# Padding between the weight sub-tiles, and feed-forward matmuls that read their tokens backwards

## The chip, the cores and the metric

One core of a Trainium2 chip runs the whole program. The metric is the device time of one execution in microseconds (us). TensorE is written PE in the views of the profile, its weight loads PEld; VectorE is DVE, ScalarE is ACT, GpSimd is POOL and SyncE is SP.

## The reference

Input `x` has 8 sequences of 512 tokens with 256 features. Two residual blocks follow each other. The first is a recurrent block (projections, 8 exponential moving averages along the tokens, gates, a layer norm). The second is a mixture of feed-forward networks (FFNs), in which nearly all of the arithmetic lies:

```python
def _dense(x, wi, wo):
    return jax.nn.relu(x @ wi) @ wo          # 256 -> 1024 -> 256
s0 = _dense(hidden_states, share_wi[0], share_wo[0])
s1 = _dense(hidden_states, share_wi[1], share_wo[1])
s2 = _dense(hidden_states, share_wi[2], share_wo[2])
...
expert_out = out_a * wa + out_b * wb         # two of four experts, picked for each sequence
g = jax.nn.softmax(jax.nn.relu(gi @ gate_w1) @ gate_w2, axis=-1)
out = expert_out * g[:, 0, None, None] + s0 * g[:, 1, None, None] + s1 * g[:, 2, None, None] + s2 * g[:, 3, None, None]
```

Each sequence thus passes five FFNs: three shared ones and two experts. Everything is float32.

## The kernel before

The work goes sequence by sequence. Features lie on the 128 partitions (256 features are `CT` = 2 tiles), tokens along the free dimension. Each float32 operand is split into a high and a low part of type float32r, and a product is three matmuls: high by high, low weights by high data, high weights by low data.

An FFN of one sequence has 8 slots (`TPF`), one for each 128 of the 1024 hidden features; five FFNs make 40 slots (`SLOTS`). A slot has an `up` and a `down`, and `mixture` of the TensorE program (line 744) runs `up` two slots (`LAG`) ahead of `down`.

- `up` (line 668) makes one bank of `ps_up` with six matmuls. For each of two feature tiles, line 695 multiplies the high weights and line 696 the low weights with `x2_hi`; `up_rest` (line 665) multiplies the high weights with `x2_lo`, twice. All 512 tokens are the moving operand.
- ScalarE applies relu and writes `hid_hi` (line 1065, function `relu`), VectorE writes the rest `hid_lo` (line 1306).
- `down` (line 705) makes both banks of `ps_down` with six matmuls: lines 737 and 738 with `hid_hi` for each of two output tiles, then line 741 twice with `hid_lo`. Again the tokens are the moving operand. (Line 730 does one of these in the last slot.)

The last sequence runs two of the FFNs in halves of 256 tokens (`LAST_PASSES`); there the weights of the last slots lie in `xg_hi_all`, `xg_lo_all`, `ct_hi`, `ct_lo`, `wc_hi`, `wc_lo` and `x2_*_all` (`again_wi`, `again_wo`), and one pass writes to `ps_aux`.

Before each matmul TensorE loads 128x128 weights, beside the matmul before it. The weights of half an FFN are a unit: `wi` and `wo` have two buffers of [high part, low part] each, and a part has `CT * UF` = 1024 or `UT * E` = 1024 elements in a partition (4096 bytes). SyncE's queue brings them from a scratch in DRAM that holds the split weights: `load_wi` (line 532) and `load_wo` (line 539), one transfer of 8192 bytes in a partition each. During the first sequence the weights are split on the chip and stored there by `keep_wi` (line 505) and `keep_wo` (line 511).

The recurrent block of the next sequence is woven between the slots by plans (`PLAN_TENSOR` and its like, lines 50 to 120), through `ps_aux` and with weights in `wc_hi` and `wc_lo`. Its moving operands `xg_hi` and `xg_lo` start after a margin of `EDGE` = 128 zero elements in each feature tile; one element of the margin is read (`gate_product`, line 770). For the second sequence the same product reads `x1_hi` and `x1_lo` from the tail of `x2_hi_all` and `x2_lo_all`, with a margin `EDGE1` = 16.

The tensors lie in a partition one after the other in the order of lines 193 to 250. From their sizes: the first is at byte 1152, `wi` at 17536, `wo` at 33920, `hid_hi` at 66688, `wc_hi` at 83072, `x2_hi_all` at 151680, `x2_lo_all` at 160384, `xg_hi_all` at 177280, and the last ends at 228996 (a partition has 229376 bytes). Every start named here leaves 128 when it is divided by 512, and so does each tile of 128 weights and each row of 512 tokens in `wi`, `wo`, `hid_hi`, `hid_lo`, `x2_hi`, `x2_lo`, `xg_hi` and `xg_lo`. The exceptions are `x1_hi` and `x1_lo`: their two feature tiles start at remainders 192 and 256.

Of the kernel before, what the change touches and what calls it, by code (L numbers as in the profile page):

```python
# [10 lines left out]
F32R = mybir.dt.float32r  # L11
# [3 lines left out]
P = 128  # L15
B, T, E = 8, 512, 256
CT = E // P
# [9 lines left out]
UF = F // 2  # L27
UT = UF // P
# [4 lines left out]
NU = 4  # L33
# [66 lines left out]
for _d in range(D):  # L100
# [25 lines left out]
               (4, slice(HALF, T)), (3, slice(HALF, T)))  # L126
LAST_SLOTS = len(LAST_PASSES) * TPF
AGAIN = LAST_SLOTS - TPF
EDGE = 128
EDGE1 = 16  # L130

AUX_BANKS = {"mod_hidden": (0,), "mod": (1,), "gate_hidden": (0,)}
GATING = {"gate_hidden", "gate_part_hi", "gate_part_lo", "gate_logits", "gate_exp", "gate_part", "gate_soft",
          "mix0", "mix1", "mix2", "mix3", "store", "store0", "store1", "final_scale", "final_expert_a", "final_expert_b",
          *(f"final_early{i}" for i in range(NS + 1)), *(f"final_late{i}" for i in range(NS))}


def later(count):
# [32 lines left out]
def build(nc, x, w_ctx, params, types_row, types_all, shared_wi, shared_wo, expert_wi, expert_wo,  # L171
# [3 lines left out]
    split_wi = nc.dram_tensor("split_wi", [KEPT, 2, P, 2 * CT * UF], F32, kind="Internal").ap()  # L175
    split_wo = nc.dram_tensor("split_wo", [KEPT, 2, P, 2 * UT * E], F32, kind="Internal").ap()

    with ExitStack() as ctx:
        def sb(name, shape, dt=F32):
            return ctx.enter_context(nc.sbuf_tensor(name, shape, dt))  # L180
# [7 lines left out]

        raw_wi = sb("raw_wi", [P, 2, CT * UF])
        raw_wo = sb("raw_wo", [P, 2, UT * E])  # L190
        wi = sb("wi", [P, 2, 2, CT * UF], F32R)
        wo = sb("wo", [P, 2, 2, UT * E], F32R)
        ex = sb("ex", [P, 2, 2, CT * UF])
        hid_hi = sb("hid_hi", [P, NU, T], F32R)
        hid_lo = sb("hid_lo", [P, NU, T], F32R)
# [55 lines left out]
        ps_up = [ctx.enter_context(nc.psum_tensor(f"ps_up{i}", [P, T], F32)) for i in range(NU)]  # L251
# [130 lines left out]
        def f32(ap):  # L382
            return ap.bitcast(F32)
# [34 lines left out]
        def half(h):  # L418
            return slice(h * HALF, (h + 1) * HALF)

        def col(c, i=0):
            return par[:, c + i:c + i + 1]

# [48 lines left out]
        def _(sp):  # L472
# [26 lines left out]
            def kept_place(split, u):  # L499
                ffn, half = u // 2, u % 2  # L500
                if ffn < NS:
                    return split[ffn, half]
                return split[bass.ds(expert["now"] + ffn, 1), half].rearrange("o p f -> (o p) f")

            def keep_wi(u):

                sp.wait_ge(wi_ready, u + 1)
                sp.dma_start(kept_place(split_wi, u), f32(wi[:, u % 2, :, :]).rearrange("p s f -> p (s f)"))\
                    .then_inc(wi_kept[u % 2], 16)

            def keep_wo(u):

                sp.wait_ge(wo_ready, u + 1)
                sp.dma_start(kept_place(split_wo, u), f32(wo[:, u % 2, :, :]).rearrange("p s f -> p (s f)"))\
                    .then_inc(wo_kept[u % 2], 16)

            def split_source(kept, of, b, u):
# [14 lines left out]
            def load_wi(b, u):  # L532
                b, u, count, buf = unit_of(b, u)
                source = split_source(wi_kept, split_wi, b, u)

                sp.wait_ge(up_done, (count - 1) * UT)
                sp.dma_start(f32(wi[:, buf, :, :]).rearrange("p s f -> p (s f)"), source).then_inc(wi_landed[buf], 16)

            def load_wo(b, u):
                b, u, count, buf = unit_of(b, u)  # L540
                source = split_source(wo_kept, split_wo, b, u)

                sp.wait_ge(down_done, (count - 1) * UT)
                sp.dma_start(f32(wo[:, buf, :, :]).rearrange("p s f -> p (s f)"), source).then_inc(wo_landed[buf], 16)

            def load_again_wi(half):

# [107 lines left out]
        def _(pe):  # L655
# [6 lines left out]
            def up_rest(ps, w_hi, parity, tokens):  # L662

                for c in range(CT):
                    mm = pe.matmul(ps, w_hi[c], x2_lo[:, parity, c, tokens], start=False, stop=c == CT - 1)  # L665
                return mm

            def up(b, at, parity, tokens=None, done=True, last=False):

                k, part = slot_of(at, last)  # L670
                opens = tokens is not None
                tokens = tokens or part
                u, j = k // UT, k % UT
                if k == 0 and tokens.stop == T and not opens:
                    pe.wait_ge(x2_hi_ready, b)
                if j == 0 and b == 0:
                    pe.wait_ge(wi_ready, u + 1)
                if j == 0 and b > 0 and at < SLOTS:
                    pe.wait_ge(wi_landed[u % 2], 16 * ((b - 1) * (UNITS // 2) + u // 2 + 1))
                if j == 0 and at >= AGAIN:  # L680
                    pe.wait_ge(again_loaded[u % 2], 64)

                ps = ps_up[at % NU][:, tokens]

                def weights(c):
                    if at >= AGAIN:
                        return [w[:, c, j * P:(j + 1) * P] for w in again_wi[u % 2]]
                    cols = slice(c * UF + j * P, c * UF + (j + 1) * P)
                    return wi_hi[:, u % 2, cols], wi_lo[:, u % 2, cols]

                for c in range(CT):
                    w_hi, w_lo = weights(c)
                    if opens and k == 0:
                        pe.wait_ge(open_x2_hi, tokens.start // HALF * CT + c + 1)
                    pe.matmul(ps, w_hi, x2_hi[:, parity, c, tokens], start=c == 0, stop=False)  # L695
                    pe.matmul(ps, w_lo, x2_hi[:, parity, c, tokens], start=False, stop=False)  # L696
                if opens and tokens.start == 0:
                    return
                elif k == 0 and tokens.stop == T:
                    pe.wait_ge(x2_split, b + 1)  # L700
                mm = up_rest(ps, [weights(c)[0] for c in range(CT)], parity, tokens)
                if done:
                    mm.then_inc(up_done, 1)

            def down(b, at, last=False):

                k, tokens = slot_of(at, last)
                u, j = k // UT, k % UT
                ffn = k // TPF
                if j == 0 and b == 0:  # L710
                    pe.wait_ge(wo_ready, u + 1)
                if j == 0 and b > 0 and at < SLOTS:
                    pe.wait_ge(wo_landed[u % 2], 16 * ((b - 1) * (UNITS // 2) + u // 2 + 1))
                w_hi, w_lo = again_wo[u % 2] if at >= AGAIN else (wo_hi[:, u % 2, :], wo_lo[:, u % 2, :])
                pe.wait_ge(hid_hi_ready, b * SLOTS + (at + 1))
                banks = []
                for c in range(CT):
                    cols = slice(j * E + c * P, j * E + (c + 1) * P)

                    if k % TPF == 0 and ffn == 0 and later(b * 2):  # L720
                        pe.wait_ge(experts_ready, b * 2 - (1 - c))
                    if k % TPF == 0 and ffn > 0 and at < SLOTS:
                        pe.wait_ge(y_ready, b * 8 + (2 * ffn - 1 + c))
                    if at == AGAIN:
                        pe.wait_ge(experts_ready, b * 2 + 1 + c)
                    start, stop = k % TPF == 0, k % TPF == TPF - 1
                    bank = ps_down[c][:, tokens]
                    if at == LAST_SLOTS - 1 and c == 1:
                        pe.wait_ge(hid_ready, b * SLOTS + (at + 1))
                        pe.matmul(banks[0][0], banks[0][1], hid_lo[:, at % NU, tokens], start=False, stop=True)\  # L730
                            .then_inc(last_down, 1)
                        banks = []
                    if SLOTS <= at < AGAIN:
                        bank = ps_aux[1][:, c * HALF:(c + 1) * HALF]
                        start, stop = start and c == 0, stop and c == CT - 1
                    banks.append((bank, w_hi[:, cols], stop))
                    pe.matmul(bank, w_hi[:, cols], hid_hi[:, at % NU, tokens], start=start, stop=False)  # L737
                    pe.matmul(bank, w_lo[:, cols], hid_hi[:, at % NU, tokens], start=False, stop=False)  # L738
                pe.wait_ge(hid_ready, b * SLOTS + (at + 1))
                for bank, w, stop in banks:  # L740
                    mm = pe.matmul(bank, w, hid_lo[:, at % NU, tokens], start=False, stop=stop)  # L741
                mm.then_inc(down_done, 1)

            def mixture(b, k, parity, last):
# [212 lines left out]
            def opening():  # L957
# [53 lines left out]
                    up(0, k, 0, half(0), done=False)  # L1011
                pe.wait_ge(open_x2_split, 1)
                for k in range(LAG):
                    up_rest(ps_up[k][:, half(0)], [wi_hi[:, 0, c * UF + k * P:c * UF + (k + 1) * P] for c in range(CT)], 0, half(0))
                open_turn_back(1)
                next_x_terms(ps_aux[1], W_SOMA, 1).then_inc(open_x1_done, 1)
                for k in range(LAG):
# [847 lines left out]
```

## Time and profile before

| | |
|---|---|
| time, median of 2 runs | 1045.24 us (1045.14 and 1045.34) |
| span of the profiled execution, first to last instruction | 1044.1 us |
| its mean granted TensorE clock | 0.999 of full |
| TensorE matmul busy | 1036.7 us, 99% |
| TensorE weight loads busy | 861.1 us, 82% |
| VectorE, ScalarE, GpSimd busy | 756.8, 405.0, 16.3 us |
| moved by DMA | 223.02 MB, mean 214 GB/s |

The profiled execution has its span in the page; its own time outside the profiler is not listed, and the two times shown stand 1.0 and 1.2 us above the span. A matmul's recorded duration holds the time in which its results drain, so matmuls overlap in the records and the distance from one start to the next is what counts. Where the timeline merges two or more matmuls (x2), the second starts inside the row.

### The profile page before, as it was taken

The page shows a single profiled execution, that of the slowest core. Times are in us where ns is not written, and L with a number is a line of the kernel's source. Part 1 is how long each engine was busy: PE and PEld are TensorE (multiplying, and loading weights), DVE is VectorE, ACT ScalarE, POOL GpSimd, SP SyncE. Part 2 cuts the span into 40 slices and gives each one's busy share as a digit, 9 for nine tenths or more (in the row PEclk, how much of TensorE's full clock was granted, in tenths as well). Part 3 has the DMA queues.
Part 4 walks back from the last instruction along what each step waited for, and adds up shares of the span by engine and source line. Part 5 has one row for each costly group of instructions (what it writes and reads, how often), then busy time and mean ns, then how long its engine had stood idle before and what let it go on. Part 6 is the DMA issues. An engine that isn't in the chain of part 4 may idle for free.

```text
span 1044.1 us, 12751 instructions
## 1 busy us (share of the span) xinstructions
PE 1036.7 (99%) x4850; PEld 861.1 (82%) x4850; DVE 756.8 (72%) x1260; ACT 405.0 (39%) x663; POOL 16.3 (2%) x26
## 2 busy tenths in 40 slices
PE   8999999999999999999999999999999999999998
PEld 5688888888888888888888888888888888888898
DVE  6989977799547986389764996559955599545236
ACT  8654555423443234422344223433334432423232
POOL 1200000000000000000000000000000000000000
PEclk9999999999999999999999999999999999999999
DMA  5388999786354754466544664546645465355582
GB/s 213 121 313 275 312 356 356 282 324 240 131 192 167 257 181 162 162 238 210 197 164 163 231 235 152 185 162 242 208 154 201 163 235 204 146 201 191 203 323 90
DMA packets 38302, 223.02 MB, mean 214 GB/s; under 512 B 4514, under 2 KB 5282, under 8 KB 16610
## 3 DMA queue, kind: packets, MB, share of 16 engines
q1 hardware_dynamic: 35938, 209.63, 56.1%
q0 software_dynamic: 2304, 12.58, 3.2%
q8 instruction: 38, 0.62, 0.2%
q14 instruction: 22, 0.18, 0.0%
HBM read 188.51 MB, written 33.69 MB: 213 GB/s over the span
## 4 chain that ended last, share of the span: by engine, by line
PE 96%; DMA 2%; DVE 2%; issue 0%; SPq 0%; ACT 0%; DVEq 0%
PE ps_up L665 14%; PE ps_up L695 14%; PE ps_up L696 14%; PE ps_down L737 14%; PE ps_down L741 14%; PE ps_down L738 14%; PE ps_aux L658 2%; PE ps_aux L659 2%; PE ps_aux L660 2%; DMA wi<-split_wi 1%; DVE y L1633 1%; PE ps_aux L837 1%; PE ps_aux L834 1%; PE ps_aux L833 1%; PE ps_aux L822 1%; PE ps_aux L818 1%
## 5 line engine op out<-in xcount | busy, mean ns | idle before, releaser
L1065 ACT ACTIVATE hid_hi<-ps_up 128x512 fp32r<-128x512 f32 (+1 forms) x336 | 193.5, 576 | 507.8 <-PE ps_up L665 507.6
L1306 DVE SCALAR_TENSOR_TENSOR hid_lo<-ps_up,hid_hi 128x512 fp32r<-128x512 f32 (+1 forms) x336 | 220.1, 658 | 228.9 <-ACT hid_hi L1065 227.5
L695 PE MATMUL ps_up<-x_hi_all,wi 128*128 128x512 f32 (+1 forms) x660 | 250.8, 382 | 0.4 <-DMA wi<-split_wi 0.4
L696 PE MATMUL ps_up<-x_hi_all,wi 128*128 128x512 f32 (+1 forms) x660 | 249.9, 380 | 0.0
L737 PE MATMUL ps_down<-hid_hi,wo 128*128 128x512 f32 (+1 forms) x640 | 245.3, 384 | 0.1
L738 PE MATMUL ps_down<-hid_hi,wo 128*128 128x512 f32 (+1 forms) x640 | 245.1, 384 | 0.0
L665 PE MATMUL ps_up<-x_lo_all,wi 128*128 128x512 f32 (+1 forms) x660 | 197.4, 380 | 0.2 <-DVE x_lo_all L1297 0.2
L741 PE MATMUL ps_down<-hid_lo,wo 128*128 128x512 f32 (+1 forms) x640 | 193.9, 384 | 0.0
L695 PEld LDWEIGHTS ps_up<-x_hi_all,wi 128*128 128x128 f32 x660 | 124.1, 188 | 24.1 <-DMA wi<-split_wi 0.8
L696 PEld LDWEIGHTS ps_up<-x_hi_all,wi 128*128 128x128 f32 x660 | 124.1, 188 | 23.0
L665 PEld LDWEIGHTS ps_up<-x_lo_all,wi 128*128 128x128 f32 x660 | 122.0, 188 | 24.3 <-DVE x_lo_all L1297 0.4
L737 PEld LDWEIGHTS ps_down<-hid_hi,wo 128*128 128x128 f32 x640 | 120.2, 188 | 24.7 <-issue 0.2
L738 PEld LDWEIGHTS ps_down<-hid_hi,wo 128*128 128x128 f32 x640 | 120.2, 188 | 23.5
L741 PEld LDWEIGHTS ps_down<-hid_lo,wo 128*128 128x128 f32 x640 | 119.0, 188 | 24.0 <-DVE hid_lo L1306 0.3
L1416 DVE TENSOR_TENSOR_SCAN trace<-alpha,trace 128x512 f32<-128x512 f32 x98 | 119.1, 1216 | 0.0
L1450 DVE SCALAR_TENSOR_TENSOR trace<-modb,blend_w,gates 128x512 f32<-128x512 f32 x98 | 68.9, 744 | 0.0
L1459 DVE TENSOR_TENSOR temporal<-trace,temporal 128x512 f32<-128x512 f32 x98 | 62.1, 676 | 0.0
L1373 DVE SCALAR_TENSOR_TENSOR x<-y,g,x 128x512 f32<-128x512 f32 x56 | 38.9, 746 | 0.2
L658 PE MATMUL ps_aux<-xg_hi_all,wc_hi 128*128 128x512 f32 x88 | 34.5, 392 | 0.0
L659 PE MATMUL ps_aux<-xg_lo_all,wc_hi 128*128 128x512 f32 x88 | 34.3, 389 | 0.0
L660 PE MATMUL ps_aux<-xg_hi_all,wc_lo 128*128 128x512 f32 x88 | 34.2, 389 | 0.0
L1078 ACT ACTIVATE y<-ps_down 128x512 f32<-128x512 f32 x48 | 26.1, 596 | 18.5 <-PE ps_down L741 18.5
(248 smaller groups left out, 855.1 us busy)
## 6 DMA issues: line engine op xcount, KB each, us to landing
wi<-split_wi SPq DMA_DIRECT2D x70, 1024.0 KB, 4.8
wo<-split_wo SPq DMA_DIRECT2D x70, 1024.0 KB, 4.9
modb<-mod_scratch SPq DMA_DIRECT2D x28, 512.0 KB, 4.6
split_wi<-wi SPq DMA_DIRECT2D x10, 1024.0 KB, 7.3
split_wo<-wo SPq DMA_DIRECT2D x10, 1024.0 KB, 7.6
xt<-in_x SPq DMA_DIRECT2D x8, 512.0 KB, 5.8
split_wi<-ex POOLq DMA_DIRECT2D x4, 1024.0 KB, 8.6
split_wo<-ex POOLq DMA_DIRECT2D x4, 1024.0 KB, 6.0
```

The costliest lines, as they stand in the source:

```text
L658: pe.matmul(ps, w_hi, x_hi, start=start, stop=False)
L665: mm = pe.matmul(ps, w_hi[c], x2_lo[:, parity, c, tokens], start=False, stop=c == CT - 1)
L695: pe.matmul(ps, w_hi, x2_hi[:, parity, c, tokens], start=c == 0, stop=False)
L696: pe.matmul(ps, w_lo, x2_hi[:, parity, c, tokens], start=False, stop=False)
L737: pe.matmul(bank, w_hi[:, cols], hid_hi[:, at % NU, tokens], start=start, stop=False)
L738: pe.matmul(bank, w_lo[:, cols], hid_hi[:, at % NU, tokens], start=False, stop=False)
L741: mm = pe.matmul(bank, w, hid_lo[:, at % NU, tokens], start=False, stop=stop)
L1065: act.activation(hid_hi[:, k % NU, tokens], ps_up[k % NU][:, tokens], ACT.Relu).then_inc(hid_hi_ready, 1)
L1306: dve.scalar_tensor_tensor(hid_lo[:, k % NU, tokens], ps_up[k % NU][:, tokens], 0.0, f32(hid_hi[:, k % NU, tokens]), ALU.max, ALU.subtract ...
L1416: scan = dve.tensor_tensor_scan(trace_of(d)[:, c, :], alpha[:, d:d + 1].broadcast_to([P, T]), trace_of(d)[:, c, :], 0.0, ALU.mult, ALU.add)
L1450: dve.scalar_tensor_tensor(trace_of(d)[:, c, :], modb[:, d // 2 % 2, d % 2, :], blend_w[:, c, d:d + 1], gates[:, c, :], ALU.mult, ALU.mult ...
L1459: dve.tensor_tensor(temporal[:, c, :], trace[:, c, :], temporal[:, c, :], ALU.add).then_inc(ema_sum, 1)
```

## The change

`wi` gets 32 unused elements (128 bytes) after each part, `wo` 16 (64 bytes). The margin `EDGE` shrinks from 128 to 96. The transfers that fill or store `wi` and `wo` move two pieces of 4096 bytes in a partition in place of one of 8192. All FFN matmuls take the token slice with step -1 from the last to the first: `up` so leaves `ps_up` in reversed order, relu and its rest keep that order, and `down` reverses it again. Where the first sequence's opening does halves of the tokens, `up` writes to the mirrored half of the bank.

```diff
-EDGE = 128
+EDGE = 96
+WI_PAD = 32
+WO_PAD = 16
...
+def back(tokens):
+
+    return slice(tokens.stop - 1, tokens.start - 1 if tokens.start else None, -1)
...
-        wi = sb("wi", [P, 2, 2, CT * UF], F32R)
-        wo = sb("wo", [P, 2, 2, UT * E], F32R)
+        wi = sb("wi", [P, 2, 2, CT * UF + WI_PAD], F32R)[:, :, :, 0:CT * UF]
+        wo = sb("wo", [P, 2, 2, UT * E + WO_PAD], F32R)[:, :, :, 0:UT * E]
...
+        def mirrored(tokens):
+            return slice(T - tokens.stop, T - tokens.start)
...
-                sp.dma_start(f32(wi[:, buf, :, :]).rearrange("p s f -> p (s f)"), source).then_inc(wi_landed[buf], 16)
+                sp.dma_start(f32(wi[:, buf, :, :]), source.rearrange("p (s f) -> p s f", s=2)).then_inc(wi_landed[buf], 16)
...
-                    mm = pe.matmul(ps, w_hi[c], x2_lo[:, parity, c, tokens], start=False, stop=c == CT - 1)
+                    mm = pe.matmul(ps, w_hi[c], x2_lo[:, parity, c, back(tokens)], start=False, stop=c == CT - 1)
...
-                ps = ps_up[at % NU][:, tokens]
+                ps = ps_up[at % NU][:, mirrored(tokens) if opens else tokens]
...
-                    pe.matmul(ps, w_hi, x2_hi[:, parity, c, tokens], start=c == 0, stop=False)
-                    pe.matmul(ps, w_lo, x2_hi[:, parity, c, tokens], start=False, stop=False)
+                    pe.matmul(ps, w_hi, x2_hi[:, parity, c, back(tokens)], start=c == 0, stop=False)
+                    pe.matmul(ps, w_lo, x2_hi[:, parity, c, back(tokens)], start=False, stop=False)
...
-                    pe.matmul(bank, w_hi[:, cols], hid_hi[:, at % NU, tokens], start=start, stop=False)
-                    pe.matmul(bank, w_lo[:, cols], hid_hi[:, at % NU, tokens], start=False, stop=False)
+                    pe.matmul(bank, w_hi[:, cols], hid_hi[:, at % NU, back(tokens)], start=start, stop=False)
+                    pe.matmul(bank, w_lo[:, cols], hid_hi[:, at % NU, back(tokens)], start=False, stop=False)
...
-                    mm = pe.matmul(bank, w, hid_lo[:, at % NU, tokens], start=False, stop=stop)
+                    mm = pe.matmul(bank, w, hid_lo[:, at % NU, back(tokens)], start=False, stop=stop)
```

`keep_wi`, `keep_wo` and `load_wo` change as `load_wi` does, and line 730 as the last line shown.

## Rows read from the trace of the kernel before

**Rows 1.** The page: busy time of each engine, the 40 slices, the clock
```profile
PE 1036.7 (99%) x4850; PEld 861.1 (82%) x4850; DVE 756.8 (72%) x1260; ACT 405.0 (39%) x663; POOL 16.3 (2%) x26
...
PE   8999999999999999999999999999999999999998
...
PEclk9999999999999999999999999999999999999999
```

**Rows 2.** The page: the chain that ended last, its shares by engine
```profile
PE 96%; DMA 2%; DVE 2%; issue 0%; SPq 0%; ACT 0%; DVEq 0%
```

**Rows 3.** Groups by line, TensorE: count, busy us, mean ns, idle before
```profile
L695 PE MATMUL ps_up<-x_hi_all,wi 128*128 128x512 f32 (+1 forms) x660 | 250.8, 382 | 0.4 <-DMA wi<-split_wi 0.4
L696 PE MATMUL ps_up<-x_hi_all,wi 128*128 128x512 f32 (+1 forms) x660 | 249.9, 380 | 0.0
L737 PE MATMUL ps_down<-hid_hi,wo 128*128 128x512 f32 (+1 forms) x640 | 245.3, 384 | 0.1
...
L658 PE MATMUL ps_aux<-xg_hi_all,wc_hi 128*128 128x512 f32 x88 | 34.5, 392 | 0.0
...
L738 PE MATMUL ps_aux<-hid_hi,wo 128*128 128x256 f32 x16 | 4.2, 284 | 0.0
...
L922 PE MATMUL ps_up<-ident,modb 128*128 128x128 f32 x32 | 4.0, 273 | 0.0
...
L696 PE MATMUL ps_up<-x_hi_all,ct_lo 128*128 128x256 f32 x8 | 2.1, 283 | 0.0
```

**Rows 4.** Timeline of TensorE, 498.5 to 501.8 us: start, duration
```profile
498.32 0.39 PE L696 MATMUL ps_up<-x_hi_all,wi 128*128 128x512 f32 x1
498.55 0.39 PE L695 MATMUL ps_up<-x_hi_all,wi 128*128 128x512 f32 x1
...
501.49 0.39 PE L696 MATMUL ps_up<-x_hi_all,wi 128*128 128x512 f32 x1
```

**Rows 5.** Timeline of TensorE in the opening: float32 matmuls, not float32r
```profile
22.23 1.91 PE L922 MATMUL ps_up<-ident,modb 128*128 128x128 f32 x16
...
31.04 7.03 PE L893 MATMUL ps_down<-y,gw 128*128 128x512 f32 x16
...
37.48 0.59 PE L893 MATMUL ps_down<-y,gw 128*128 128x512 f32 x1
```

**Rows 6.** Timeline of TensorE around the product with `x1` (margin 16)
```profile
60.40 0.40 PE L658 MATMUL ps_aux<-x_hi_all,wc_hi 128*128 128x512 f32 x1
60.63 0.40 PE L659 MATMUL ps_aux<-x_lo_all,wc_hi 128*128 128x512 f32 x1
60.87 0.39 PE L660 MATMUL ps_aux<-x_hi_all,wc_lo 128*128 128x512 f32 x1
...
65.94 0.39 PE L695 MATMUL ps_up<-x_hi_all,wi 128*128 128x512 f32 x1
```

**Rows 7.** DMA issues by destination: count, KB each, median us to landing
```profile
wi<-split_wi SPq DMA_DIRECT2D x70, 1024.0 KB, 4.8
wo<-split_wo SPq DMA_DIRECT2D x70, 1024.0 KB, 4.9
modb<-mod_scratch SPq DMA_DIRECT2D x28, 512.0 KB, 4.6
```

**Rows 8.** The chain that ended last, 205 to 230 us: the one late load
```profile
211.87 0.47 PE ps_up L665 x2
212.34 0.02 issue
212.35 12.53 DMA wi<-split_wi
```

**Rows 9.** Waits: ScalarE for TensorE, VectorE for ScalarE: us, times, longest
```profile
ACT hid_hi L1065 <- PE ps_up L665: 507.6, 297, 6.7
DVE hid_lo L1306 <- ACT hid_hi L1065: 227.5, 152, 4.5
```

More of the change, by code:

```diff
@@ L507, in keep_wi @@
                 sp.wait_ge(wi_ready, u + 1)
-                sp.dma_start(kept_place(split_wi, u), f32(wi[:, u % 2, :, :]).rearrange("p s f -> p (s f)"))\
+                sp.dma_start(kept_place(split_wi, u).rearrange("p (s f) -> p s f", s=2), f32(wi[:, u % 2, :, :]))\
                     .then_inc(wi_kept[u % 2], 16)
@@ L513, in keep_wo @@
                 sp.wait_ge(wo_ready, u + 1)
-                sp.dma_start(kept_place(split_wo, u), f32(wo[:, u % 2, :, :]).rearrange("p s f -> p (s f)"))\
+                sp.dma_start(kept_place(split_wo, u).rearrange("p (s f) -> p s f", s=2), f32(wo[:, u % 2, :, :]))\
                     .then_inc(wo_kept[u % 2], 16)
@@ L543, in load_wo @@
                 sp.wait_ge(down_done, (count - 1) * UT)
-                sp.dma_start(f32(wo[:, buf, :, :]).rearrange("p s f -> p (s f)"), source).then_inc(wo_landed[buf], 16)
+                sp.dma_start(f32(wo[:, buf, :, :]), source.rearrange("p (s f) -> p s f", s=2)).then_inc(wo_landed[buf], 16)
             def load_again_wi(half):
@@ L729, in down @@
                         pe.wait_ge(hid_ready, b * SLOTS + (at + 1))
-                        pe.matmul(banks[0][0], banks[0][1], hid_lo[:, at % NU, tokens], start=False, stop=True)\
+                        pe.matmul(banks[0][0], banks[0][1], hid_lo[:, at % NU, back(tokens)], start=False, stop=True)\
                             .then_inc(last_down, 1)
@@ L1013, in opening @@
                 for k in range(LAG):
-                    up_rest(ps_up[k][:, half(0)], [wi_hi[:, 0, c * UF + k * P:c * UF + (k + 1) * P] for c in range(CT)], 0, half(0))
+                    up_rest(ps_up[k][:, half(1)], [wi_hi[:, 0, c * UF + k * P:c * UF + (k + 1) * P] for c in range(CT)], 0, half(0))
                 open_turn_back(1)
```

## The prediction

> **What bounds the kernel now.** I read the page first: TensorE is busy for 1036.7 of 1044.1 us, in every slice from the second to the last but one at nine tenths or more, at full clock (2.4 GHz) [rows 1]. The chain that ended last is TensorE for 96% [rows 2]. ScalarE waits for TensorE's `up` 297 times and 507.6 us in all, and VectorE in turn for ScalarE [rows 9]: they are ahead and wait. So the time is the number of matmuls times their distance, and I asked the timeline for that distance. From 498.32 to 501.49 us there are 14 steps, 226.4 ns each [rows 4] (with the rounding of the starts, 226 to 227; I use 226.7). 512 columns at 2.4 GHz are 213.3 ns. So each float32r matmul costs some 13.4 ns more than its columns. Float32 matmuls cost less on top: each of their passes runs at half the column rate, and 15 steps from 31.04 to 37.48 us are 429.3 ns each, where 512 columns at 1.2 GHz are 426.7; the 128-column ones have 15 steps in 1.91 - 0.27 us (one takes 273 ns), 109 ns each, against 106.7 [rows 3, 5]. They have the same weight loads, and only some 2.5 ns on top. So about 10.9 ns of a float32r matmul seem to come from two streams that both read the same memory, the tokens at double rate and the next weights beside them. This surplus is what the change can move, in either sense.
>
> A third row says that the surplus depends on where the operands lie. The product with `x1` has 24 matmuls of 512 columns between 60.40 and 65.94 us [rows 6]. That is 230.8 ns each, 4.1 more than in rows 4. They differ in one thing that I can see: their tokens start 64 or 128 bytes (one element less in half of them) off the remainder (mod 512) that all weights share.
>
> **How many matmuls it touches.** Lines 695, 696 and 665 have 660 each, lines 737, 738 and 741 640 each: 3900; the smaller groups of these lines, with other weights or banks, are three of 16 and twelve of 8, of which one each is shown, 144 together [rows 3]. That is 4044 of 4850 records, 2028 of `up` and 2016 of `down`, most with 512 columns.
>
> **The change part by part.**
>
> Padding. I worked out the new places from the sizes. `wi` still starts at remainder 128 (mod 512); its four parts now start at 128, 256, 384 and 0. `wo` starts at 128 too (`wi` grew by 512), its parts are at 128, 192, 256 and 320. `wo` grew by 256, so all behind it, `hid_hi`, `hid_lo`, `x2_hi`, `x2_lo`, `wc_hi` and `wc_lo`, moves to 384. If only the remainder mod 256 matters, a token row (128) agrees with high `wi` in both buffers and high `wo` in the first. High weights are 4 of 6 loads. Then a third of `up` (676) and two thirds of `down` (1344) are off, 2020 matmuls, at 4.1 ns [rows 6]: +8.3 us. If it is mod 512, only high `wi` of the second buffer agrees: two thirds of `up` and all of `down`, 3368, +13.8 us. I take 8.3, because the rows show a cost for shifts of 64 and 128 bytes and none for 256. From below: nothing excludes that a distance that no row has costs less than the present one; the nearest row is the float32 surplus of 2.5 ns [rows 5], 10.9 ns less on 4044: -44 us. From above, 230.8 need not be the worst.
>
> Margin. `xg_hi` and `xg_lo` have three lines with 88 matmuls, 264 [rows 3]. Their rows now start at 256 and 128 (high) and at 0 and 384 (low), against weights at 384: half of them off mod 256, 132 at 4.1 ns, +0.5 us. The shrink is what lets the padding fit: 768 bytes more would end the last tensor at 229764, past 229376; with 512 fewer it ends at 229252.
>
> Backwards tokens. No row has a moving operand with step -1. What it adds in instructions is nothing. Its price has bounds far apart. Below: it could turn a crossing of the two streams into a parallel run and save the 10.9 ns, the same -44 us as above (not twice). Above: the row at half column rate [rows 5], 429 instead of 227 ns, +202 ns on 4044 (less on the few with 256 columns), about +800 us. I take zero, the row nearest to it being the same matmul read forwards [rows 4]: four consecutive elements are the same bytes in either order, and the bank that is written and relu see no change of order in their own addresses.
>
> As to that, the Trainium skill ("SBUF — State Buffer", Specifications) says that SBUF works in 16-byte cachelines and an access stream keeps its rate with two hits in each. A reversed float32 row has four, so by that rule the reversal is free; no row of this trace shows a reversed stream.
>
> Transfers. The count of DMAs and their place on SP's queue stay. Each `wi` or `wo` load has twice the pieces at half the size. Loads of 1024 KB in 8192-byte pieces land in 4.8 us; `modb` moves 512 KB in pieces of 2048 bytes in 4.6 [rows 7]. If 4096-byte pieces moved at that lower rate, a load would take at most 9.2 us. A buffer is refilled while the four slots of the other one run, 12 matmuls each at 0.227 us: 10.9 us. So it stays hidden at either end in the steady part. It isn't hidden where the queue is full: at 212 us a load took 12.53 us and TensorE idled 0.4 us [rows 3, 8]. A few per cent more there costs another 0.3 us; the bound, if the early loads all slow down, is some 4 us. I take 0.3. If the surplus falls instead, a slot shrinks by 0.13 us of 2.72 and the same covers hold.
>
> Sum: 1044.1 + 8.3 + 0.5 + 0.3 = 1053.2 us of span. The median of the runs stands 1.1 us above the span of the profiled execution; with that, 1054.3 us.
>
> **The rivals.**
>
> *The surplus goes.* The weights and the tokens now run so that they seldom want the same bytes of a line. For it: the surplus exists, it belongs to the double-rate stream, and it moves with the operands' places [rows 4 to 6]. Against it: the places now differ from part to part, so no single good distance is chosen, and the only other distances that the trace has cost more. Price: between all of it, 4044 x 10.9 = 44 us (1001 us), and half of it (1023 us); 1012 us in the middle.
>
> *Nothing moves.* The surplus is a fixed price of a float32r weight swap, and the 4.1 ns of rows 6 have another cause in that busy stretch. Price: the 0.3 us of transfers, 1045.5 us. In the Trainium skill ("TensorE: Matmul & The Clock Gate", Part 2) the engine has one read port for the moving operand and an independent one for the weights, so that a load takes no bandwidth from the running matmul; by that rule the places and the direction are nothing and the time stays. Its 2.5 ns on top of N/2.4 would also be the whole surplus: float32 passes agree with it (429 ns), float32r ones, at 226.7, don't.
>
> *The streams run together (slower).* If the weights are read from the last column to the first, the reversed tokens now move in the same direction at twice the pace, catch up with them, and queue behind them instead of crossing. Where: in the first half of every FFN matmul. Price: a load of 128 columns reads for some 107 ns [rows 5]; tokens held to half rate for all of it lose 53 ns in each matmul, +216 us; held for a quarter of it, 13.3 ns, +54 us, 1099 us. It decides from 5.2 ns in each matmul on (21 us). For it: the surplus behaves like a conflict. Against it: no row tells in which order weights are read.
>
> *Backward reads at half rate (slower).* The double rate may need two neighbours in rising order. Then 512 columns take 429 ns as in rows 5, and the time is some 1045 + 800 = 1845 us. This is the case in which the change doesn't do what it says. For it: only that no row shows the opposite.
>
> **How the numbers follow.** Misplaced parts at the old surplus, my forecast: 0.32, of which 0.30 ends below 1066 us. Surplus goes: 0.30, of which 0.28 is over 2% (below 1024.3 us). Nothing moves: 0.11. Streams together: 0.20. Half rate: 0.07. Over 2% is about what a measurement of this kernel can tell from no change. Faster: 0.28. Slower: 0.02 + 0.20 + 0.07 = 0.29. Within 2%: 0.30 + 0.02 + 0.11 = 0.43. The forecast's own range is 1047 to 1066 us. The range for 8 in 10 leaves out the half rate, the upper half of the streams together and the very end of the surplus: 1003 to 1110 us.
>
> **What would show it.** In the changed profile the distance of FFN matmuls in the timeline is the whole answer. Right: 226.7 ns where a matmul's tokens and the next weights agree mod 256, and some 231 elsewhere, different from part to part. Wrong: one distance near 216 to 221 everywhere (surplus gone), 227 everywhere (nothing moves), 240 or more (together), 429 (half rate). For the smaller terms: PE idle before line 695 from `wi` loads above 1 us would show the transfers mis-sized, and a landing time of `wi` far from 5 us too.

## The result and the profile after

The changed kernel takes 1069.9 us (median of 2 runs, 1069.4 and 1070.4) against 1045.24 before: ratio 1.0238, with its 95% interval 1.0208 to 1.0267. It is slower by over 2%. I had forecast 1054.3 us and "within 2%" as the likeliest outcome; the time lies in the stated range of 1003 to 1110 us. It is just above the part of it that I had for my forecast (1047 to 1066 us), and where I had put "the streams run together" (21 us and more above the old time), but the mechanism is neither's, as the experiments show.

The page of the kernel after answers to [rows 1, 2]:

```profile
PE 1060.5 (99%) x4850; PEld 861.8 (81%) x4850; DVE 758.0 (71%) x1260; ACT 404.6 (38%) x663; POOL 16.3 (2%) x26
...
PE   8999999999999999999999999999999999999998
...
PEclk9999999999999999999999999999999999999999
...
PE 97%; DVE 2%; DMA 1%; issue 0%; SPq 0%; ACT 0%; DVEq 0%
```

TensorE is what bounds it, now too, at the same clock, with the same 4850 matmuls. Its busy time grew by 23.8 us (1060.5 - 1036.7), the span by 23.6 (1067.7 - 1044.1). So the waits didn't grow in sum: the matmuls themselves stand further apart. Nor is it the loads' own length: PEld is 861.8 us against 861.1.

The timeline of TensorE after, in the same stretch as [rows 4] (line 705 is line 695 of before; all lines behind the diff's first part are shifted by 10):

```profile
505.72 0.40 PE L705 MATMUL ps_up<-x_hi_all,wi 128*128 128x512 f32 x1
...
508.52 0.40 PE L705 MATMUL ps_up<-x_hi_all,wi 128*128 128x512 f32 x1
...
514.12 0.40 PE L705 MATMUL ps_up<-x_hi_all,wi 128*128 128x512 f32 x1
```

From one slot's first matmul to the next one's are 12 steps: 2.80 us, 233.3 ns each, and 8.40 us for 36. Inside the slots it is the same, whichever part of `wi` or `wo` is loaded. I had asked the timeline to choose between 226.7 ns mixed with 231 by part, one value of 216 to 221, 227 everywhere, and 240 or more. It shows one value everywhere in this stretch, but 233, which is none of the four.

The view of stretches says the same for the middle of the run. Columns: stretch, its length, then busy us and number of instructions of PE, PEld, DVE, ACT, POOL, the clock, the DMA share and GB/s. First before, then after:

```profile
400.00:1000.00 600.00, 599.93 (x2739) 499.53 (x2738) 407.11 (x673) 208.96 (x333) 0.00 (x0) 1.00 0.54 193
```

```profile
400.00:1000.00 600.00, 600.00 (x2661) 487.33 (x2660) 406.01 (x675) 204.90 (x323) 0.00 (x0) 1.00 0.53 187
```

2739 matmuls in 600 us became 2661, 219.1 ns each became 225.5 (all kinds and sizes together).

Where the whole difference lies can be added up. With the shapes kept apart, the groups of the six FFN lines hold 3 x 604 and 3 x 608 = 3636 matmuls of 512 columns, in both kernels. Over the pairs of these that follow each other directly in the records with less than 250 ns between their starts (3575 before, 3577 after) the mean distance from start to start is 226.93 ns before and 233.46 after. The difference times 3636 is 23.7 us, as much as the whole loss. The FFN passes with 256 columns didn't grow (119.8 ns before, 119.0 after). I use this mean, "the mean distance", for every kernel below; it moves by 0.1 to 0.2 ns with the limit at which a step counts as a wait, so hundredths mean nothing in it. What is left nearly cancels: the other products with 512 columns, untouched by the reversal, take 1 us more, and the steps above 250 ns, which hold the waits, change by less than that in sum.

The smaller terms, in the groups by line and in the DMA issues (columns: count, KB each, median us to landing) of the kernel after:

```profile
L705 PE MATMUL ps_up<-x_hi_all,wi 128*128 128x512 f32 (+1 forms) x660 | 255.8, 390 | 0.4 <-DMA wi<-split_wi 0.4
```

```profile
wi<-split_wi SPq DMA_DIRECT2D x70, 1024.0 KB, 5.2
wo<-split_wo SPq DMA_DIRECT2D x70, 1024.0 KB, 5.2
```

The smaller pieces cost a load 0.3 to 0.4 us [rows 7]. TensorE idles 0.4 us for `wi`, the same sum as before [rows 3], but for another load. The late one of before, at 212 us [rows 8], no longer delays it. The chain that ended last has a new one, in the last sequence, where the FFNs run in halves:

```profile
1021.18 6.55 DMA wi<-split_wi
1027.73 0.04 issue
1027.77 0.39 PE ps_up L705
```

Four slots of 12 matmuls with 256 columns last 5.7 us there (119.0 ns each), and this load took 6.55. pad_only, below, waits at the same place (0.3 us for `wi`, behind a load of 6.52 us); back_only, whose loads move in pieces of 8192 bytes, has no wait for `wi` at all. So the smaller pieces aren't quite hidden.

ScalarE and VectorE still wait for TensorE (536.9 us in 303 waits, against 507.6 in 297 [rows 9]). The product with `x1` is unmoved, 24 steps in 5.54 us, 230.8 ns, as in [rows 6]:

```profile
60.16 0.40 PE L668 MATMUL ps_aux<-x_hi_all,wc_hi 128*128 128x512 f32 x1
...
65.70 0.40 PE L705 MATMUL ps_up<-x_hi_all,wi 128*128 128x512 f32 x1
```

### The profile page after: what moved, and what is told of

Its sections match the earlier page's. It is cut to its first block, busy times and chain, and to the rows that moved or that the text cites. A ratio compares the mean times of both kernels' runs of the same rounds, so it can differ in the third digit from the quotient of the medians.

```text
span 1067.7 us, 12751 instructions
## 1 busy us (share of the span) xinstructions
PE 1060.5 (99%) x4850; PEld 861.8 (81%) x4850; DVE 758.0 (71%) x1260; ACT 404.6 (38%) x663; POOL 16.3 (2%) x26
## 4 chain that ended last, share of the span: by engine, by line
PE 97%; DVE 2%; DMA 1%; issue 0%; SPq 0%; ACT 0%; DVEq 0%
PE ps_up L705 14%; PE ps_up L675 14%; PE ps_up L706 14%; PE ps_down L747 14%; PE ps_down L748 14%; PE ps_down L751 14%; PE ps_aux L668 2%; PE ps_aux L670 2%; PE ps_aux L669 2%; DVE y L1643 1%; PE ps_aux L843 1%; PE ps_aux L847 1%; PE ps_aux L844 1%; DMA wi<-split_wi 1%; PE ps_aux L827 1%; PE ps_aux L828 1%
## 5 line engine op out<-in xcount | busy, mean ns | idle before, releaser
L1075 ACT ACTIVATE hid_hi<-ps_up 128x512 fp32r<-128x512 f32 (+1 forms) x336 | 193.5, 576 | 537.3 <-PE ps_up L675 536.9
L705 PE MATMUL ps_up<-x_hi_all,wi 128*128 128x512 f32 (+1 forms) x660 | 255.8, 390 | 0.4 <-DMA wi<-split_wi 0.4
L706 PE MATMUL ps_up<-x_hi_all,wi 128*128 128x512 f32 (+1 forms) x660 | 254.8, 388 | 0.0
L747 PE MATMUL ps_down<-hid_hi,wo 128*128 128x512 f32 (+1 forms) x640 | 250.3, 392 | 0.1
L748 PE MATMUL ps_down<-hid_hi,wo 128*128 128x512 f32 (+1 forms) x640 | 250.0, 392 | 0.0
L675 PE MATMUL ps_up<-x_lo_all,wi 128*128 128x512 f32 (+1 forms) x660 | 201.7, 388 | 0.2 <-DVE x_lo_all L1307 0.2
L751 PE MATMUL ps_down<-hid_lo,wo 128*128 128x512 f32 (+1 forms) x640 | 198.2, 392 | 0.0
```

The source lines that it names most:

```text
L675: mm = pe.matmul(ps, w_hi[c], x2_lo[:, parity, c, back(tokens)], start=False, stop=c == CT - 1)
L705: pe.matmul(ps, w_hi, x2_hi[:, parity, c, back(tokens)], start=c == 0, stop=False)
L706: pe.matmul(ps, w_lo, x2_hi[:, parity, c, back(tokens)], start=False, stop=False)
L747: pe.matmul(bank, w_hi[:, cols], hid_hi[:, at % NU, back(tokens)], start=start, stop=False)
L748: pe.matmul(bank, w_lo[:, cols], hid_hi[:, at % NU, back(tokens)], start=False, stop=False)
L751: mm = pe.matmul(bank, w, hid_lo[:, at % NU, back(tokens)], start=False, stop=stop)
```

## The experiments

My theory after the result: reading the tokens from the last to the first has a price of its own, 6.6 ns in each 512-column matmul, and the padding adds little to it. The rivals: the padding costs it and the order of the tokens is free (my forecast, with more parts misplaced than I counted); or the reversed tokens run in the same direction as the weight reads and so get in their way ("the streams run together").

### First: the two halves of the change

**pad_only** takes the reversal out of the changed kernel:

```diff
-    return slice(tokens.stop - 1, tokens.start - 1 if tokens.start else None, -1)
+    return tokens
...
-            return slice(T - tokens.stop, T - tokens.start)
+            return tokens
```

> The changed kernel with its padding and margin, but tokens read forwards. Theory P (the places cost, the direction nothing): 230 to 233.3 ns from one FFN matmul to the next, and 1060 to 1070 us. Theory D (the direction costs, the places nothing): 226.7 ns and 1045 to 1047 us. My forecast's own step (226.7 ns where tokens and weights agree mod 256, 230.8 elsewhere): two distances, and 1054 us.

**back_only** takes the padding out:

```diff
-EDGE = 96
-WI_PAD = 32
-WO_PAD = 16
+EDGE = 128
+WI_PAD = 0
+WO_PAD = 0
```

> The changed kernel with no padding and the margin of 128, tokens read backwards. Theory P: 226.7 ns and 1045 us. Theory D: 233.3 ns and 1069 to 1070 us. If the padding was meant to soften what the direction costs: more than 233.3 ns, over 1070 us.

Measured: pad_only 1060.7 us, ratio 1.0143 [1.0126, 1.0159]; back_only 1067.9 us, ratio 1.0214 [1.0197, 1.0231]; before, on the same chip, 1045.6. The timelines of pad_only and, under it, back_only:

```profile
504.96 0.39 PE L705 MATMUL ps_up<-x_hi_all,wi 128*128 128x512 f32 x1
...
506.35 0.39 PE L747 MATMUL ps_down<-hid_hi,wo 128*128 128x512 f32 x1
...
507.75 0.39 PE L705 MATMUL ps_up<-x_hi_all,wi 128*128 128x512 f32 x1
```

```profile
505.15 0.40 PE L705 MATMUL ps_up<-x_hi_all,wi 128*128 128x512 f32 x1
...
507.95 0.40 PE L705 MATMUL ps_up<-x_hi_all,wi 128*128 128x512 f32 x1
...
513.55 0.40 PE L705 MATMUL ps_up<-x_hi_all,wi 128*128 128x512 f32 x1
```

Each half is slower alone, both intervals leave out 1 (pad_only is slower by less than 2%), and they don't add: +15.1 and +22.3 us alone, +24.7 together. That the padding adds little holds only beside the reversal; alone it costs 15.1 us, which my theory didn't have. back_only has the uniform 233.3 ns of the changed kernel (2.80 us for 12 steps, 8.40 for 36), so the distance after is that of backward reading. The padding is then worth the 2.0 us between 1067.9 and 1069.9, or 2.4 if each is taken against its own before; the two intervals overlap, so the times alone don't show it. The spans of the two traces differ by 1.6 us: 0.07 ns on 3636 FFN matmuls is 0.3 us of it, the other 512-column products with `wc_hi` and its like, whose margin moved, went from a mean of 229.1 to 230.5 ns, some 0.5 us over 371 recorded pairs, and the late load shown above makes two steps longer by 0.6 us. (Before, these products stood at 227.8 ns. So 1.3 ns came with the reversal alone, which doesn't touch them.)

In pad_only the distance differs by part, as forecast, between 226 and 239 ns, with a mean of 231.28. But the matmuls whose operands still agree mod 256 aren't spared: where the next weights are high `wo` of the first buffer (remainder 128, tokens at 384) the steps beside `hid_hi` are 226, 227, 235 or 236 ns, 231.2 in the mean. 4.35 ns on all 3636 is 15.8 us, which is what it costs. So counting misplaced parts was the wrong count. That a step depends on its neighbours too is my reading of it; no run takes them apart.

### Second: does it hang on the weight reads?

**half_lo_forward** (kernel before) and **half_lo_back** (back_only) load and multiply only 64 of 128 output features in the two lines with the low weights; the other 64 lose their low-weight term. (All kernels from here on are single runs, but for the three that have an interval in the table of the last part.)

```diff
-                    pe.matmul(ps, w_lo, x2_hi[:, parity, c, tokens], start=False, stop=False)
+                    pe.matmul(ps[0:H1], w_lo[:, 0:H1], x2_hi[:, parity, c, tokens], start=False, stop=False)
```

> The kernel before, but the matmuls with low weights (696 and 738, a third of the FFN's) load and compute 64 of the 128 output features, so the low term of the other 64 is left out. If the surplus of 13.3 ns over the columns comes from the weight load that runs beside a matmul, the matmul before such a line gets shorter by some 6 ns, the others stay at 226.7, about 1037 us in all. If it is a fixed price of each float32r matmul: 226.7 everywhere and 1045 us.

> As half_lo_forward (the low term of 64 of 128 output features is left out), with tokens backwards and no padding. If the 6.6 ns of backward reading are a conflict with the weight load, both shrink beside the half load: some 223 ns before a line 706 or 748, 233 elsewhere. If backward reading has a price of its own, the distance before those lines stays 6.6 ns above that of half_lo_forward.

Measured: 1054.6 us forwards, 1069.2 us backwards, mean distance 229.80 and 233.39 ns. Forwards a shorter load made the kernel slower, which neither of my two cases had. The steps beside the half loads stay at 227.3 ns in the mean; those that begin with a half-wide matmul, and the one between the two matmuls with low data, take some 232. I read it so that the 226.9 ns of before belong to a regular sequence and are lost in an irregular one, but no run shows that by itself. Backwards the length of the load changes nothing.

**same_w_forward** and **same_w_back** make every FFN load (but the one of line 730 of before) read one column of weights 128 times, so that the weight stream stays in one place (the products are of that column alone):

```diff
+            def one(w):
+                return w[:, 0:1].broadcast_to([P, P])
...
-                    pe.matmul(ps, w_hi, x2_hi[:, parity, c, tokens], start=c == 0, stop=False)
+                    pe.matmul(ps, one(w_hi), x2_hi[:, parity, c, tokens], start=c == 0, stop=False)
```

> The kernel before, but each FFN weight load reads the first of its 128 columns 128 times (so all outputs of an FFN matmul are one feature's). The load has the same length but touches only one place. If the surplus of 13.3 ns is a conflict between the load's reads and the tokens' reads in memory: less, down to 215.8 ns a matmul and about 1000 us. If loads have no part in it: 226.7 ns and 1045 us.

> As same_w_forward (all outputs of an FFN matmul are one feature's), tokens backwards, no padding. If the 20 ns of backward reading are a conflict with the load's reads: below 226 ns. If backward reading has a price of its own, whatever the load does (as the half loads say): 233.3 ns and 1066 to 1068 us.

**same_token** is the mirror of it: the weights as before, and each FFN matmul reads its first token over and over (`broadcast_to` on the tokens), forwards; the output is that of one token.

> The kernel before, but each FFN matmul reads its first token 512 times in place of 512 tokens (so all tokens of an FFN get the first one's result). Weight loads as before. If the surplus comes from fetching new lines of tokens: 213.3 to 216 ns and about 1000 us. If it is in the array or the start of each matmul: 226.7 ns and 1045 us.

Measured, with 1044.3 us for the kernel before: same_w_forward 1058.1 us, mean distance 230.64 ns; same_w_back 1067.1 us, 233.31 ns; same_token 1020.4 us, 217.33 ns. Timelines of same_w_back and of same_token:

```profile
504.91 0.40 PE L709 MATMUL ps_up<-x_hi_all,wi 128*128 128x512 f32 x1
...
507.71 0.40 PE L709 MATMUL ps_up<-x_hi_all,wi 128*128 128x512 f32 x1
```

```profile
504.82 0.38 PE L699 MATMUL ps_up<-x_hi_all,wi 128*128 128x512 f32 x1
...
506.99 0.38 PE L699 MATMUL ps_up<-x_hi_all,wi 128*128 128x512 f32 x1
```

same_w_forward is slower than either of my two cases for it. Two readings follow. A weight stream that doesn't move can't run along with the tokens, and 233.3 ns stay (12 steps in 2.80 us): "the streams run together" is out. And with tokens that don't move the distance falls to 217.0 ns (10 steps in 2.17 us), some parts to 215. So 9.6 of the 13.6 ns of surplus of the kernel before go away when all columns read the same token; that the fetching of new places makes them is the likely reason, not a tested one, since the data differ too. That is the one kernel here that gets rid of them, and it computes something else.

### Third: place and size

**shift_256** and **shift_64** put a gap of 256 or 64 bytes ahead of `hid_hi` in the kernel before, so that the FFN tokens shift against `wi` and `wo`; **back_shift_64** does the latter in back_only.

```diff
+        sb("gap", [P, 64])
         hid_hi = sb("hid_hi", [P, NU, T], F32R)
```

> The kernel before with an unused gap of 256 bytes ahead of hid_hi, so that all tokens of the FFNs lie 256 bytes (mod 512) off the weights' remainder, forwards. My forecast took a shift by 256 to cost nothing: 226.7 ns and 1045 us. If places agree only mod 512: some 230.8 ns and 1059 us.

> The kernel before with a gap of 64 bytes ahead of hid_hi, tokens forwards. If a shift by 64 costs what the rows with x1 showed: some 230.8 ns and 1059 us. If the padding's cost came from parts that differ among each other and a shift common to all is free: 226.7 ns and 1045 us.

> Tokens backwards, no padding, and a gap of 64 bytes ahead of hid_hi, so that all FFN tokens lie 64 bytes off the weights' remainder. If backward reading costs the same at any place: 233.3 ns and 1066 to 1068 us. If the place mod 256 matters backwards too: another distance, 227 to 240 ns.

Measured: shift_256 1045.5 us (the kernel before, beside it, 1044.3) and 226.9 ns, the distance of before; shift_64 1051.5 us and 228.99 ns (the kernel before, beside it, 1046.5); back_shift_64 1068.3 us and 233.33 ns. Forwards the place counts, and a shift of 256 is free, as I had assumed for the sum; these are two shifts, and others weren't tried. The shift of 64 costs 2.1 ns, half of the 4.1 that I had taken from the product with `x1`. Backwards a shift of 64 costs nothing.

**cols384_forward** and **cols384_back** do only 384 of 512 tokens in each FFN matmul; the last 128 tokens are left out.

> The kernel before, but the FFN matmuls of 512 tokens do the first 384 only (the FFN of 128 tokens is left out). 384 columns at 2.4 GHz are 160 ns. If the forward surplus of 13.3 ns belongs to each matmul: 173.3 ns. If it belongs to the columns read: 170 ns.

> As cols384_forward (the FFN of 128 tokens is left out), tokens backwards, no padding. If the backward surplus of 20 ns is paid once for each matmul: 180 ns. If it is paid by the column (20 of 213.3 ns): 175 ns.

Measured: 962.0 and 966.7 us, mean distance 174.11 and 177.97 ns. Here TensorE waits now and then (182.8 us busy of the 200 from 400 us on, forwards), so that the distance tells more than the time. 384 columns are 160 ns. So forwards the surplus is the same as with 512 columns (14.1 against 13.6 ns): a price of the matmul and not of its columns. Backwards it is 18.0 ns against 20.1, and with 256 columns (106.7 ns) 11.8 against 13.1 forwards, from back_only and the kernel before. So backward reading costs nothing at 256 columns, 3.9 ns at 384 (most steps there are 173 ns forwards and 176 backwards, with a good part at 181 and 182) and 6.5 at 512; neither "fixed" nor "per column" describes it.

### Fourth: which order costs?

My reason for taking zero had been that four elements are the same 16 bytes in either order. The reversal also changes the order in which these 16-byte groups come. Six kernels without padding, each with another order of the tokens, applied twice, so that the result is in order. All take back_only and turn the token slice in another way. lines_back has groups of 4 tokens from the last to the first, rising inside:

```diff
-def back(tokens):
-    return slice(tokens.stop - 1, tokens.start - 1 if tokens.start else None, -1)
+def turned(ap):
+    return ap.rearrange("p (a b) -> p a b", b=4)[:, ::-1, :]
...
-                    pe.matmul(ps, w_hi, x2_hi[:, parity, c, back(tokens)], start=c == 0, stop=False)
+                    pe.matmul(ps, w_hi, turned(x2_hi[:, parity, c, tokens]), start=c == 0, stop=False)
```

eights_back, sixteens_back and halves_swap have `b=8`, `16` and `64` (32, 64 and 256 bytes; the blocks of 256 start 128 bytes past a multiple of 256, as the tokens do). inside_back ends in `[:, :, ::-1]`, the groups in order and last to first inside. pairs_swap swaps the two 16-byte groups of each 32 bytes:

```diff
-    return ap.rearrange("p (a b) -> p a b", b=4)[:, ::-1, :]
+    return ap.rearrange("p (a g b) -> p a g b", g=2, b=4)[:, :, ::-1, :]
```

> No padding, margin 128 as before. The FFN matmuls visit their tokens in groups of four (16 bytes), the groups from the last to the first, inside a group in rising order; again twice over, so the result is in order. If the price of reading backwards (6.7 ns on a 512-column matmul) belongs to the order in which the 16-byte groups are fetched: 233 ns, 1067 us. If it belongs to the falling order of the elements inside such a group, or to the single step of -4 bytes: 226.7 ns, 1045 us. If short runs of a stream cost something of their own: above 233 ns.

> The other half of the reversal: the groups of four tokens in rising order, inside a group from the last to the first. If the order of the 16-byte groups is what costs: 226.7 ns, 1045 us. If the falling order inside a group, or the step of -4 bytes, is what costs: 233 ns, 1067 us. If any access pattern of two levels costs: both this and the one before are slow, and by the same amount.

> Groups of 64 tokens (256 bytes) visited from the last to the first, rising inside: only 7 jumps in a matmul of 512 tokens, each of a multiple of 256 bytes. If only a stream that falls all the way costs: 226.7 ns, 1045 us. If a pattern of two levels costs something fixed: the same price as in the two before. If each jump costs a little: between 227 and 233 ns.

> As lines_back (1068.1 us), with groups of 8 tokens (32 bytes) visited from the last to the first, rising inside: half of the steps from one 16-byte line to the next rise. If every falling step between lines costs: about half of lines_back's 6.7 ns, 230 ns, 1056 us. If a falling order costs as soon as it is finer than some size: either 233.3 ns (1067 us) or 226.7 ns (1045 us).

> Groups of 16 tokens (64 bytes) visited from the last to the first: one step between lines in four falls. If every falling step costs: 228.4 ns, 1051 us. If there is a size from which it is free, and 64 bytes is at or above it: 226.7 ns, 1045 us, as with 256 bytes.

> The two 16-byte lines of each 32 bytes swapped, the pairs themselves in rising order: half of the steps between lines fall, yet the stream as a whole rises. If each falling step between lines costs, or lines must be asked for one after the other: 230 ns or more, 1056 us or more. If only the direction of the whole stream, against the weight reads, counts: 226.7 ns, 1045 us.

| kernel | bytes in a group | groups | time, us | ratio to before, interval | mean distance, ns |
|---|---|---|---|---|---|
| inside_back | 16 | rising, elements falling inside | 1045.1 | 1.0000 [0.9991, 1.0010] | 226.93 |
| halves_swap | 256 | falling | 1045.1 | 0.9999 [0.9990, 1.0009] | 226.93 |
| sixteens_back | 64 | falling | 1069.1 (one run) | | 233.35 |
| eights_back | 32 | falling | 1068.4 (one run) | | 233.39 |
| lines_back | 16 | falling | 1068.1 | 1.0221 [1.0204, 1.0238] | 233.38 |
| pairs_swap | 16 | rising, neighbours swapped | 1066.8 (one run) | | 233.16 |

The kernel before took 1045.2 us beside the three with intervals and 1046.8 beside the other three. The timelines of lines_back, inside_back, sixteens_back, pairs_swap and halves_swap:

```profile
505.35 0.40 PE L705 MATMUL ps_up<-x_hi_all,wi 128*128 128x512 f32 x1
...
508.15 0.40 PE L705 MATMUL ps_up<-x_hi_all,wi 128*128 128x512 f32 x1
```

```profile
505.62 0.39 PE L705 MATMUL ps_up<-x_hi_all,wi 128*128 128x512 f32 x1
...
506.98 0.39 PE L747 MATMUL ps_down<-hid_hi,wo 128*128 128x512 f32 x1
```

```profile
506.97 0.40 PE L706 MATMUL ps_up<-x_hi_all,wi 128*128 128x512 f32 x1
...
509.77 0.40 PE L706 MATMUL ps_up<-x_hi_all,wi 128*128 128x512 f32 x1
```

```profile
505.56 0.39 PE L705 MATMUL ps_up<-x_hi_all,wi 128*128 128x512 f32 x1
...
508.36 0.39 PE L705 MATMUL ps_up<-x_hi_all,wi 128*128 128x512 f32 x1
```

```profile
505.78 0.39 PE L705 MATMUL ps_up<-x_hi_all,wi 128*128 128x512 f32 x1
...
507.14 0.39 PE L747 MATMUL ps_down<-hid_hi,wo 128*128 128x512 f32 x1
```

12 steps take 2.80 us in the first, third and fourth (233.3 ns); six take 1.36 in the second and fifth (226.7 ns). The table splits the reversal cleanly. Elements falling inside 16 bytes are free, so my reason holds as far as it goes. A pattern of two levels is free. Blocks of 256 bytes in falling order are free. Every order tried that breaks the rising order in blocks of 64 bytes or less pays the whole price at once: one step in four falling (sixteens_back) as much as all of them (lines_back), so the price isn't one per falling step. pairs_swap tells the most: the stream as a whole still rises, and it pays nearly all of it, so it isn't the direction of the stream either. In pairs_swap and eights_back the steps aren't uniform: most are near 231 or near 236 ns, and only their mean is 233. 128 bytes weren't tried, so the limit lies somewhere between 64 and 256.

All this is at 512 columns. In the passes with 256 columns the same kernels have 119.8 ns (before), 119.9 (eights_back), 118.3 (lines_back), 117.8 (sixteens_back) and 114.3 (pairs_swap). There no order costs anything, and swapping neighbours saves 5.5 ns.

## Why the prediction was wrong

**What bounds the kernel**: right. TensorE alone, and the distance of FFN matmuls "is the whole answer": 6.53 ns times 3636 is the result.

**Backwards tokens, "I take zero"**: this is the step that failed. It cost 22.3 us (back_only), 6.5 ns in each FFN matmul of 512 columns. I took the nearest row, the same matmul read forwards, and added a reason that is true only inside 16 bytes (inside_back). I never asked what the reversal does to the order of the 16-byte groups, which is what costs (lines_back). The rule I quoted from the Trainium skill ("SBUF — State Buffer", Specifications), that a stream with two hits in each 16-byte line keeps its rate, gives zero for back_only and lines_back, which have four hits; both cost 6.5 ns per matmul, so here the measurement decides against it. For inside_back rule and trace agree, with 226.93 ns.

**Padding, +8.3 us**: mis-sized; alone it costs 15.1 us (pad_only). I counted 2020 matmuls whose parts don't agree mod 256, at 4.1 ns each. Measured are 4.35 ns in the mean over all 3636, also on steps whose parts agree. That the two sizes look alike is chance: the one is a mean over all, and a shift of all tokens by 64 bytes costs 2.1 ns (shift_64). The bound that I gave for mod 512, 13.8 us, came near, for a wrong reason: a shift by 256 is free (shift_256). In the changed kernel most of this term never shows, since it doesn't add to the reversal. So it is luck that the 8.3 us bring my sum nearer to the result, and luck as well that the time lies in my range: the range is wide for the sake of other mechanisms.

**That the terms add up**: they don't (15.1 and 22.3 alone, 24.7 together). I had stated this nowhere as an assumption, and it was one.

**Margin +0.5 us**: padding and margin together raise the mean of the other 512-column products from 227.8 to 229.6 ns forwards (pad_only against before) and from 229.1 to 230.5 backwards, 0.7 and 0.5 us. The size is about right; no run has the margin alone. **Transfers +0.3 us**: loads land in 5.2 in place of 4.8 us. The size is about right (0.4 us of idling; against back_only, two steps are 0.6 us longer), but the place isn't. I looked for it in the full queue at 212 us, and that wait went away. It came in the last sequence, for which I had worked out no cover: four slots with 256 columns last 5.7 us, the load took 6.55. In the steady part the cover held.

**The rivals.** "The surplus goes" is out for this change, but not in principle: 9.6 ns of the surplus go away in same_token. "Nothing moves" is out. "The streams run together" named the right side and a price of 5.2 ns or more per matmul, but its mechanism falls: a weight stream that stands still (same_w_back) or is half as long in a third of the loads (half_lo_back) leaves 233.3 ns. "Half rate" is out: 233 ns, not 429.

What stays open: what inside the chip makes the order of the 16-byte groups matter, from which block size on it is free, and why backward reading costs nothing at 256 columns and 6.5 ns at 512. The runs show when the price is paid, not what is waited for.

## What to carry to other kernels

Where TensorE is busy all the time, read the distance of matmul starts to a tenth of a nanosecond before you touch an access pattern: here 6.5 ns in each of 3636 made 2.3% of the run. Of what these runs tried, a float32r matmul of 512 columns with a fresh weight load did best with its tokens read in rising 16-byte groups, and tokens and weights on the same remainder mod 256; an order that keeps whole blocks of 256 bytes, or that only turns elements inside 16 bytes, was free. Measure again at another number of columns: at 256 the orders had other prices. Work out the cover of a load anew for each part of the program in which the matmuls are shorter. And when a forecast sets an operation that no row shows at zero, list all that the operation reorders, at every size, before trusting the reason.

## What the runs showed of the hardware that I had not expected

- Less work can cost time: loading half of the low weights made the kernel 0.9% slower (1054.6 against 1045.6 us), and reading a single weight column 1.3% slower (1058.1 against 1044.3). At 256 columns it isn't so: the same two kernels have 117.7 and 116.8 ns there, against 119.8 before, and shift_64 has 116.9.
- The surplus of a float32r matmul over its columns is a fixed 13.1 to 14.1 ns forwards at 256, 384 and 512 columns, and falls to 4.0 when one token is read over and over.
- Backward reading makes the distance insensitive to everything else that was tried: padding, a shift of 64 bytes, shorter loads, loads of one column all leave 233.3 to 233.5 ns at 512 columns.
- 256 bytes come up twice: in the placement (a shift of 256 is free, one of 64 costs 2.1 ns) and in the order of fetching (blocks of 256 may fall, blocks of 64 may not). Nothing between 64 and 256 was tried in either, so whether it is one and the same size isn't shown.
